# Graph attention and expert FFN in one kernel: each chunk is routed directly behind its finishing, and source columns are queued ahead of destination rows

## The chip, the cores and the metric

The kernel runs as one program on one core of one Trainium2 chip. The core has five engines with an instruction stream each: PE (TensorE, matmuls and transposes), DVE (VectorE), ACT (ScalarE), POOL (GpSimd) and SP (SyncE, here only an issuer of DMAs). They meet only at semaphores. The metric is the device time of one execution in microseconds (us), lower is better.

## The reference

One layer has two halves. The first is a graph attention over N = 6250 nodes of D = 256 features, with 106,250 edges sorted by destination (each node has a loop). The inner function adds its own loops again.

```
xl  = layernorm(x)
q   = tanh(xl @ Wq + bq);  k = xl @ Wk + bk              # 25 columns each
w   = sum(q[s] * k[d]) / 5                                # one number per edge s -> d
ew  = exp(w - segment_max(w, d)[d]);  alpha = ew / segment_sum(ew, d)[d]
x   = x + segment_sum(alpha * xl[s], d)
```

The second is a mixture of eight experts, two per node:

```
xn = layernorm(layernorm(x)) * gamma + beta;  logits = xn @ Wr + br
the two best experts of each node, softmax over their two logits -> w_full
x  = x + sum over e of w_full[e] * (gelu(xn @ W1[e] + b1[e]) @ W2[e] + b2[e])
```

## The kernel before, in words

**Stages.** From 0 to about 100 us the kernel normalises all rows, makes q and k, writes rows of 282 numbers (features, a one, q) to `rows_dram`, and computes on the chip a list of *items*. Then comes the edge stage, about 100 to 1233 us, and then the experts, which go over blocks of 256 gathered nodes.

**An item** is two groups of 512 consecutive edges, one for each half of the nodes, each with a window of 64 destination nodes. There are 106 items. For each one:
- SP loads its 2 x 512 source numbers, column-shaped, into `idx` (`load_sources`, L357, from `srccol` on chip) and its 512 destination numbers, spread over 64 partitions twice, into `dstb` (`load_targets`, L362, from `dst_dram`). Both have XSLOTS = 4 slots.
- POOL gathers the source rows with eight indirect DMAs (L539) into one of the four slots of `xg`.
- ACT copies q out (L1240), PE transposes it (L1442), ACT copies back (L1245), PE makes scores against the keys (L1451), DVE adds the mask and takes the maximum (`maximum`, L856, L861, L868), ACT makes exponentials (L1249), PE transposes them (L1458), ACT copies (L1255), PE sums the gathered rows with them (`sums`, L1466), and DVE scales and adds into `acc` (`add_sums`, L879).
- DVE makes the mask of the *next* item behind each maximum (`edge_mask`, L846) and adds the sums of the item *before*.

In the steady order PE's sums of item n stand behind the scores of item n+1, so they come out one item late. `PEEL = 2` items are done ahead of the loops; the rest goes in quads of four items, each a loop body.

**What frees what.** A gather of item n waits for its `idx` (semaphore `s_idx`) and for the sums of item n-4 (`s_pv`), which free the slot of `xg`. An `idx` slot is free when the gather of the item that used it has landed (`s_g`). A `dstb` slot is free when the mask of its item is made (`s_mask`).

**Chunks.** The nodes lie in NCH = 7 chunks of 7 x 128. Since edges are sorted by destination, a chunk is complete after some quad; `segment(c)` loads the first and last quad of chunk c from a table that the kernel computed. DVE, PE and ACT each run a loop over chunks 0 to 5, and the last chunk follows in plain code:

```
for c in 0..5:   quads lo..hi-1;  finished(c);  one quad (hi);  route(c)
last chunk:      quads lo..hi-1;                finished(6);    route(6)
```

The line numbers of a chunk on DVE: `finished` (L904 to L930) divides `acc` by its ones column, adds x (`xr`), takes statistics, normalises into `rows`, and waits for PE's router logits (L930 adds their bias). `route` (L950 to L1020) takes the top two of eight, counts the positions of the nodes in the lists of the experts with PE's help, and adds into the list `ltok` by 14 pairs of one-hot tiles (`ab`, `bb`, L1011, L1012) that PE multiplies (L1543). On PE `finished` is transposes and logits (L1513, L1519), and at its end PE waits for L930; at the end of `route` it waits for L1020. On ACT `finished` makes the inverse deviation, copies transposes, and stores the rows of the first half of the layer (L1285, L1287); `route` makes one exponential (L1312) and stores the normalised rows (L1294); `next_rows` loads the x rows of the next chunk (L1278 to L1281) and stands between quad and `route`.

PE does the sums of the last item ahead of a stop at once (`last_sums`), and the first item of the quad behind it has no sums to do (`fresh_quad`). DVE's addition for that last item is made in the next quad.

POOL and SP have no chunks: they run one loop over all quads and are held by semaphores alone. SP's quad, which the change edits:

```
sp.wait_ge(s_mask, number(s + 1));   load_targets(sp, s, group, s + XSLOTS)
sp.wait_ge(s_g[s], ...);             load_sources(sp, s, group, s + XSLOTS)
```

Of the kernel before, what the change touches and what calls it, by code (L numbers as in the profile page):

```python
# [62 lines left out]
XSLOTS = 4  # L63
PEEL = 2
# [24 lines left out]
def build(nc, x, src, dst, Wq, bq, Wk, bk, gamma, beta, Wr, br, W1, b1, W2, b2, out):  # L89
    ctx = ExitStack()  # L90
    with ctx:
# [178 lines left out]
        s_db = [sem(f"s_db{i}") for i in range(XSLOTS)]  # L270
# [31 lines left out]
        def kept(eng, value, low, high):  # L302

            return eng.snap(eng.to_reg(value), donate=True, min_val=low, max_val=high)
# [50 lines left out]
        def load_sources(eng, s, group, a):  # L355
            for x_ in range(2):
                eng.dma_start(idx[:, s, x_, :], srccol[:, bass.ds(group(x_, a), 1), :].rearrange("p o g -> p (o g)"))\  # L357
                    .then_inc(s_idx[s], 16)

        def load_targets(eng, s, group, a):  # L360
            for x_ in range(2):
                eng.dma_start(dstb[HP * x_:HP * x_ + HP, s, :],  # L362
                              dst_dram[bass.ds(group(x_, a) * GE, GE)].partition_broadcast(HP)).then_inc(s_db[s], 16)
# [15 lines left out]
        def _(sp):  # L379
# [34 lines left out]
            sp.wait_ge(s_m0, 1)  # L414
            sp.wait_ge(s_kb, NT)
            sp.wait_ge(s_d16w, 16)
            for s in range(PEEL, XSLOTS):
                load_targets(sp, s, group, s)

            sp.dma_start(xr[0:HP, :, :], x_tiles(x, 0, CH)).then_inc(a_x, 16)  # L420
            sp.dma_start(xr[HP:P, :, :], x_tiles(x, HALF, CH)).then_inc(a_x, 16)
# [4 lines left out]
            def quad(k):  # L426
                number = counter(sp, k)
                _, _, group = item_reader(sp, k)
                for s in range(XSLOTS):
                    sp.wait_ge(s_mask, number(s + 1))  # L430
                    sp.sem_inc(tk_s, 1)
                    load_targets(sp, s, group, s + XSLOTS)
                    sp.wait_ge(s_g[s], sp.to_reg(k * (32 * G) + 32 * G))
                    sp.sem_inc(tk_s, 1)
                    load_sources(sp, s, group, s + XSLOTS)

            n_quads = quad_count(sp)
            with sp.Fori(0, n_quads) as k:
                quad(k)

            n_items = kept(sp, n_quads * 4 + PEEL, NG // 2, ITEMS)
            sp.wait_ge(s_acc, n_items + 2)
            sp.sem_inc(tk_s, 1)
            for s in range(XSLOTS):
                sp.wait_ge(s_db[s], sp.to_reg(n_quads * 32 + 32))
                sp.sem_inc(tk_s, 1)
                sp.wait_ge(s_idx[s], sp.to_reg(n_quads * 32 + 32))
                sp.sem_inc(tk_s, 1)
# [158 lines left out]
        def _(v):  # L607
# [17 lines left out]
            v.memset(ltok[:, :], 0.0).then_inc(s_v0, 1)  # L625
            v.memset(kT[:, NT * P:NTX * P], 0.0).then_inc(s_v0, 1)
            v.sem_inc(s_acc, 2)

            def statistics_0(c):

# [392 lines left out]
            with v.Fori(0, NCH - 1) as c:  # L1023
                lo, hi = segment(v, c)
                with v.Fori(lo, hi) as k:
                    quad(k)
                v.wait_ge(s_acc, v.to_reg(hi * 4 + 3))
                v.sem_inc(tk_v, 1)
                finished(c)
                with v.Fori(hi, hi + 1) as k:  # L1030
                    quad(k)
                route(c)
            lo, hi = segment(v, NCH - 1)
            with v.Fori(lo, hi) as k:
                quad(k)
# [97 lines left out]
        def _(a):  # L1133
# [162 lines left out]
            def finished(c):  # L1296


                for h, (lo_, hi_) in enumerate(((0, FIRST_PART), (FIRST_PART, CH))):
                    a.wait_ge(a_mv, CH * c + hi_)  # L1300
                    nc.scalar.activation(lnv[:, 0, lo_:hi_], mv[:, 0, lo_:hi_, 1], ACT.Ln, bias=epsc[:, 1:2], scale=1.0 + EPS)\
                        .then_inc(a_ln, 1)
                    a.wait_ge(a_ln, c * 2 + h + 1)
                    nc.scalar.activation(rstd[:, 0, lo_:hi_], lnv[:, 0, lo_:hi_], ACT.Exp, scale=-0.5).then_inc(a_rs, 1)
                for u in range(CH):
                    a.wait_ge(a_tp, c * CH + u + 1)
                    nc.scalar.copy(xnT[:, u % 2, :, :].rearrange("p c n -> p (c n)"), pb[4 + u % 2][:, 0:D]).then_inc(a_ev, 1)
                store_x2(c)

            def route(c):  # L1310
                a.wait_ge(a_df, c + 1)
                nc.scalar.activation(ex[:, :], tdiff[:, :], ACT.Exp).then_inc(a_ex, 1)  # L1312
                store_normal(c)
# [7 lines left out]
            with a.Fori(0, NCH - 1) as c:  # L1321
                lo, hi = segment(a, c)
                with a.Fori(lo, hi) as k:
                    quad(k)
                finished(c)
                with a.Fori(hi, hi + 1) as k:
                    quad(k)
                next_rows(c)
                route(c)
            lo, hi = segment(a, NCH - 1)  # L1330
            with a.Fori(lo, hi) as k:
                quad(k)
# [36 lines left out]
        def _(pe):  # L1369
# [124 lines left out]
            def fresh_quad(lo):  # L1494

                with pe.Fori(lo, lo + 1) as k:
                    quad(k, fresh=True)
# [50 lines left out]
            with pe.Fori(0, NCH - 1) as c:  # L1548
                hi = segment_quads(c)
                last_sums(PEEL + 3, counter(pe, pe.snap(hi - 1)))  # L1550
                finished(c)
                fresh_quad(hi)
                last_sums(PEEL + 3, counter(pe, hi))
                route(c)
            segment_quads(NCH - 1)
            n_items = kept(pe, quad_count(pe) * 4 + PEEL, NG // 2, ITEMS)
            sums(1, 1, pe.to_reg(n_items), pe.to_reg(n_items))
# [69 lines left out]
```

## Time and profile before

| | us |
|---|---|
| median of 3 runs | 1678.6 (1676.88 to 1678.79) |
| the profiled execution, own time | 1678.56 |
| its span | 1676.8 |
| DVE's last finishing starts (edge stage over) | 1232.73 |

| engine | busy us | share of span |
|---|---|---|
| PE | 1124.2 | 67% |
| POOL | 1101.1 | 66% |
| DVE | 827.7 | 49% |
| ACT | 519.4 | 31% |

No engine is busy all the time, and the shares mix stages: PE is at 0.9 and more in the expert stage (about the last quarter) and at 0.5 to 0.6 in the edge stage, where POOL is at 0.7 and more. POOL's busy time does not count the 0.30 us that lie between one gather and the next, so for an engine with many short instructions the busy share understates how full it is. An engine's waits are listed with their releaser; "issue" is idle time with no releaser in the profile.

### The profile page before, as it was taken

How to read it: one execution, taken by the hardware profiler on the slowest of the kernel's cores; microseconds unless marked ns; L12 is line 12 of the kernel's file. 1: busy time of each engine (PE TensorE's matmuls, PEld its weight loads, DVE VectorE, ACT ScalarE, POOL GpSimd, SP SyncE). 2: the span in 40 equal slices, each digit the busy share in tenths (PEclk: the TensorE clock that was granted, in tenths of full speed). 3: DMA queues.
4: the chain of work that ended last, by engine and by line, in shares of the span. 5: the costliest groups of instructions: out<-in, count | busy, mean ns of one | idle time of the engine just before them, and what ended most of it. 6: DMA issues, size and time to landing. Idle time of an engine off the chain costs nothing.

```text
span 1676.8 us, 30544 instructions
## 1 busy us (share of the span) xinstructions
PE 1124.2 (67%) x6718; PEld 767.1 (46%) x6719; DVE 827.7 (49%) x3273; ACT 519.4 (31%) x1474; POOL 1101.1 (66%) x1099
## 2 busy tenths in 40 slices
PE   5935655655665665556565656555647999999997
PEld 5922332423342333234232423232335888888886
DVE  7724444565466545655664565457553232322322
ACT  2522222322232323233232213222322333434332
POOL 2047777767776777677677766777703667766675
PEclk9997656666566756666676566666767999999999
DMA  9475444555456445555544564456442454544543
GB/s 200 98 170 131 129 127 128 148 145 131 129 143 159 131 127 146 150 134 143 155 130 127 141 163 113 128 147 163 124 135 44 92 98 67 99 96 94 98 69 63
DMA packets 155748, 210.05 MB, mean 125 GB/s; under 512 B 59525, under 2 KB 122589, under 8 KB 155558
## 3 DMA queue, kind: packets, MB, share of 16 engines
q0 software_dynamic: 61360, 151.84, 37.4%
q1 hardware_dynamic: 73217, 38.82, 9.7%
q10 hardware_dynamic: 21110, 18.79, 4.4%
q14 instruction: 49, 0.40, 0.1%
q8 instruction: 12, 0.20, 0.0%
HBM read 174.49 MB, written 34.41 MB: 125 GB/s over the span
## 4 chain that ended last, share of the span: by engine, by line
PE 38%; POOL 21%; issue 16%; DVE 11%; DMA 7%; DVEq 4%; ACT 3%; ACTq 1%; POOLq 0%; SPq 0%
POOL arena_a L539 20%; PE pb L1595 9%; PE pb L1587 8%; PE pb L1466 6%; DMA arena_a<-rows_dram,idx 3%; PE pb L1519 2%; PE pb L1390 2%; DVEq L314 2%; DMA arena_b<-xn_dram,gidx 2%; PE pb L1451 2%; DMA out_dram<-arena_b,tokB 2%; PE pb L1513 2%; PE pb L1442 2%; PE pb L1572 1%; PE pb L1543 1%
## 5 line engine op out<-in xcount | busy, mean ns | idle before, releaser
L539 POOL DMA_INDIRECT arena_a<-rows_dram,idx x848 | 814.3, 960 | 380.7 <-issue 257.1
L1466 PE MATMUL pb<-arena_a,arena_b 128*64 128x257 f32 x1696 | 329.9, 557 | 12.8 <-ACT arena_b L1255 12.8
L1442 PE MATMUL pb<-ident,qs 128*128 128x128 f32 x212 | 64.1, 398 | 289.5 <-ACT qs L1240 262.7
L879 DVE SCALAR_TENSOR_TENSOR acc<-acc,alpha,pb 32x257 f32 x424 | 203.3, 480 | 77.3 <-issue 67.6
L1466 PEld LDWEIGHTS pb<-arena_a,arena_b 128*64 128x64 f32 x1696 | 159.9, 196 | 142.7 <-issue 112.1
L597 POOL DMA_INDIRECT out_dram<-arena_b,tokB x104 | 166.3, 1599 | 86.0 <-DVE arena_b L1121 65.7
L1587 PE MATMUL pb<-arena_b 128*128 128x256 f32 x832 | 190.5, 383 | 1.2 <-ACT arena_b L1345 1.2
L1595 PE MATMUL pb<-arena_b 128*128 128x256 f32 x832 | 188.2, 379 | 0.0
L861 DVE CUSTOM_DVE_ANT_0 arena_b<-pb,mask,nmo 128x512 f32<-128x512 f32 x106 | 79.6, 751 | 212.5 <-PE pb L1451 203.7
L1442 PEld LDWEIGHTS pb<-ident,qs 128*128 128x128 f32 x212 | 27.5, 182 | 323.4 <-ACT qs L1240 294.1
L1587 PEld LDWEIGHTS pb<-arena_b 128*128 128x128 f32 x832 | 159.7, 192 | 23.7 <-ACT arena_b L1345 1.6
L1363 ACT ACTIVATE arena_b<-pb,b1e 128x256 f32<-128x256 f32 x208 | 98.7, 474 | 224.2 <-PE pb L1587 224.2
L1595 PEld LDWEIGHTS pb<-arena_b 128*128 128x128 f32 x832 | 154.0, 190 | 18.8
L574 POOL DMA_INDIRECT arena_b<-xn_dram,gidx x108 | 108.0, 1000 | 74.6 <-DVE gidx L1056 30.0
L1112 DVE TENSOR_TENSOR arena_b<-pb,arena_b 128x256 f32<-128x256 f32 x104 | 39.3, 420 | 222.8 <-PE pb L1595 222.8
L1249 ACT ACTIVATE arena_b<-arena_b,nbias 128x512 f32<-128x512 f32 x106 | 76.5, 721 | 224.5 <-DVE nbias L861 222.9
L1458 PE MATMUL pb<-ident,arena_b 128*128 128x128 f32 x424 | 96.9, 370 | 45.4 <-ACT arena_b L1249 44.9
L1458 PEld LDWEIGHTS pb<-ident,arena_b 128*128 128x128 f32 x424 | 62.9, 186 | 108.8 <-ACT arena_b L1249 56.5
L846 DVE TENSOR_SCALAR mask<-arena_b,win_node 64x512 bf16<-64x512 int16 x214 | 77.6, 363 | 68.4 <-issue 65.9
L1451 PE MATMUL pb<-qT,kts 25*64 25x128 f32 x1696 | 71.5, 405 | 58.6 <-ACT qT L1245 58.6
L1240 ACT COPY qs<-arena_a 128x200 f32<-128x200 f32 x106 | 38.9, 367 | 199.4 <-DMA arena_a<-rows_dram,idx 154.9
L856 DVE COPY nmo<-nm_all 32x1 f32 x424 | 61.5, 145 | 75.0 <-issue 67.7
(221 smaller groups left out, 1264.5 us busy)
## 6 DMA issues: line engine op xcount, KB each, us to landing
arena_a<-rows_dram,idx POOLq DMA_INDIRECT x848
arena_b<-dst_dram SPq DMA_DIRECT2D x212, 64.0 KB
arena_b<-in_L_ffn_W_dram SPq DMA_DIRECT2D x16, 512.0 KB, 5.0
rows_dram<-acc SPq DMA_DIRECT2D x14, 493.5 KB, 6.0
xn_dram<-arena_a ACTq DMA_DIRECT2D x7, 910.0 KB, 8.7
acc<-in_x_dram SPq DMA_DIRECT2D x13, 448.0 KB, 13.9
out_dram<-arena_a ACTq DMA_DIRECT2D x13, 448.0 KB
idx<-srccol SPq DMA_DIRECT2D x214, 2.0 KB
```

The lines of the kernel that those rows point to most:

```text
L539: g.indirect_dma_start(out=xg[:, (s * 2 + x_) * G + j, :], out_offset=None, in_=rows_dram[:, :], in_offset=bass.IndirectOffsetOnAxis(ap=id ...
L574: g.indirect_dma_start(out=xrows[:, k, :], out_offset=None, in_=xn_dram[:, :], in_offset=bass.IndirectOffsetOnAxis(ap=gidx[:, k:k + 1], ax ...
L597: g.indirect_dma_start(out=out[:, :], in_=ybuf[:, k, :], in_offset=None, out_offset=bass.IndirectOffsetOnAxis(ap=tokB[:, k:k + 1], axis=0) ...
L861: v.tensor_tensor_reduce(out=sc[:, b, :].rearrange("p (j n) -> p j n", j=G), in0=score_banks[:, :, :], in1=mask[:, b, :].rearrange("p (j n ...
L879: ins = v.scalar_tensor_tensor(out=mine, in0=mine, scalar=alpha[rows_of, b:b + 1], in1=sums_bank[b][rows_of, 0:W1COLS], op0=ALU.mult, op1= ...
L1363: nc.scalar.activation(hT[:, m, :], hidden_bank[m][:, 0:ST], ACT.Gelu, bias=b1e[:, m:m + 1]).then_inc(b_g, 1)
L1442: last = nc.tensor.transpose(pb[0][:, x_ * P:(x_ + 1) * P], qs[:, x_, :, :].rearrange("p j s -> p (j s)"), ident[:, :])
L1451: last = mm(score_banks[HP * x_:HP * x_ + HP, j, :], kts[band, HP * x_:HP * x_ + HP], qT[band, x_, :], start=True, stop=True)
L1458: last = nc.tensor.transpose(pb[2][:, j * P:(j + 1) * P], sc[:, b, j * P:(j + 1) * P], ident[:, :])
L1466: last = mm(sums_bank[b][HP * x_:HP * x_ + HP, 0:W1COLS], probT[:, b, j * P + HP * x_:j * P + HP * x_ + HP], xg[:, (s * 2 + x_) * G + j, 0 ...
L1587: last = mm(hidden_bank[m][:, 0:ST], w1s[:, b, c, m * P:(m + 1) * P], xT[:, c, :], start=c == 0, stop=c == 1, skip_group_check=True)
L1595: last = mm(pb[3 + k2][:, 0:D], hT[:, c, k2 * P:(k2 + 1) * P], w2s[:, b, c, :], start=c == 0, stop=c == 3)
```

## The change

The change has two parts.

1. On DVE, ACT and PE, `route(c)` moves to directly behind `finished(c)`. The quad that stood between them comes behind both. ACT's `next_rows(c)` stays behind the quad. The last chunk is as before.
2. On SP, each step of a quad first waits for gather n and loads source columns of item n+4, and then waits for the mask that frees a slot and loads destination rows of item n+2 (before: destination rows of item n+4, then source columns of item n+4). The mask count starts at 2, so that the same number n+1 stands for the mask of item n-2. The loads of items 2 and 3 ahead of the loop go, the loop makes them, and one load is made behind the loop; the counts waited for at the end follow.

```diff
@@ SP
             sp.wait_ge(s_d16w, 16)
-            for s in range(PEEL, XSLOTS):
-                load_targets(sp, s, group, s)
...
                 for s in range(XSLOTS):
-                    sp.wait_ge(s_mask, number(s + 1))
-                    sp.sem_inc(tk_s, 1)
-                    load_targets(sp, s, group, s + XSLOTS)
                     sp.wait_ge(s_g[s], sp.to_reg(k * (32 * G) + 32 * G))
                     sp.sem_inc(tk_s, 1)
                     load_sources(sp, s, group, s + XSLOTS)
+                    sp.wait_ge(s_mask, number(s + 1))
+                    sp.sem_inc(tk_s, 1)
+                    load_targets(sp, (s + PEEL) % XSLOTS, group, s + PEEL)
...
+            sp.wait_ge(s_mask, counter(sp, n_quads)(1))
+            sp.sem_inc(tk_s, 1)
+            _, _, group = item_reader(sp, n_quads)
+            load_targets(sp, PEEL, group, PEEL)
...
-                sp.wait_ge(s_db[s], sp.to_reg(n_quads * 32 + 32))
+                sp.wait_ge(s_db[s], sp.to_reg(n_quads * 32 + (32 if s <= PEEL else 0)))
@@ DVE
             v.sem_inc(s_acc, 2)
+            v.sem_inc(s_mask, PEEL)
...
                 finished(c)
+                route(c)
                 with v.Fori(hi, hi + 1) as k:
                     quad(k)
-                route(c)
@@ ACT
                 finished(c)
+                route(c)
                 with a.Fori(hi, hi + 1) as k:
                     quad(k)
                 next_rows(c)
-                route(c)
@@ PE
                 finished(c)
+                route(c)
                 fresh_quad(hi)
                 last_sums(PEEL + 3, counter(pe, hi))
-                route(c)
```

Line numbers of DVE, ACT and PE code are higher by 3 in the changed kernel (L930 is L933, L950 is L953).

On DVE, before the change, the end of `finished` (L930) stands directly ahead of the quad's loop (L1030), whose first work is the `nmo` copies of `maximum`:

```order
L930 TENSOR_TENSOR lg<-pb,lbias 128x56
L1030 UNCONDITIONAL_BRANCH
L1030 ISA
L314 ISA
L314 TENSOR_LOAD item_row
```

And the end of `route` (L1020) stands ahead of the jump back to the head of the chunk loop (L1023) and the loads of the segment's bounds:

```order
L1017 TENSOR_TENSOR ltok<-ltok,pb 128x408
L1020 TENSOR_TENSOR ltok<-ltok,xnT 128x408
L1023 REGISTER_ALU
L1023 COMPARE_AND_BRANCH
L341 TENSOR_LOAD segl
L341 ISA x2
L342 TENSOR_LOAD segh
```

In the changed kernel the end of `finished` (L933) is followed by the first rows of `route`:

```order
L933 TENSOR_TENSOR lg<-pb,lbias 128x56
L953 MAX top<-lg 128x8 x7
L955 ISA
L956 TENSOR_TENSOR tdiff<-top 128x7
L958 MAX_INDEX topi<-top,lg 128x8 x7
```

and the end of `route` (L1023) by the quad's loop (L1034):

```order
L1020 TENSOR_TENSOR ltok<-ltok,pb 128x408
L1023 TENSOR_TENSOR ltok<-ltok,xnT 128x408
L1034 UNCONDITIONAL_BRANCH
L1034 ISA
L314 ISA
L314 TENSOR_LOAD item_row
L314 ISA x2
```

What moved is the whole of `route`, 77 rows, over the quad; the jump back and the segment's bounds now stand behind the quad.

On SP, a step of the quad loop before the change (`arena_b<-dst_dram` are destination rows, `idx<-srccol` source columns; two of each, one per half):

```order
L304 REGISTER_ALU [waits s_mask]
L304 REGISTER_ALU
L362 ISA
L362 DMA arena_b<-dst_dram 64x512
L304 REGISTER_ALU x2
L362 ISA
L362 DMA arena_b<-dst_dram 64x512
L357 ISA [waits s_g1]
L357 DMA idx<-srccol 128x4
L357 ISA
L357 DMA idx<-srccol 128x4
```

and the same step after it:

```order
L304 REGISTER_ALU [waits s_g1]
L304 REGISTER_ALU
L357 ISA
L357 DMA idx<-srccol 128x4
L304 REGISTER_ALU x2
L357 ISA
L357 DMA idx<-srccol 128x4
L351 REGISTER_ALU
L304 REGISTER_ALU [waits s_mask]
L304 REGISTER_ALU
L362 ISA
L362 DMA arena_b<-dst_dram 64x512
```

The two pairs of DMAs have changed places with their waits.

## Rows read from the trace of the kernel before

**Rows 1.** The page: shares of the chain that ended last, and the gathers' group.

```profile
POOL arena_a L539 20%; PE pb L1595 9%; PE pb L1587 8%; PE pb L1466 6%; DMA arena_a<-rows_dram,idx 3%; PE pb L1519 2%; PE pb L1390 2%; DVEq L314 2%; DMA arena_b<-xn_dram,gidx 2%; PE pb L1451 2%; DMA out_dram<-arena_b,tokB 2%; PE pb L1513 2%; PE pb L1442 2%; PE pb L1572 1%; PE pb L1543 1%
...
L539 POOL DMA_INDIRECT arena_a<-rows_dram,idx x848 | 814.3, 960 | 380.7 <-issue 257.1
```

**Rows 2.** Waits, 240 to 1260 us: engine line, waited for, total us, times, longest us.

```profile
POOL arena_a L539 <- issue: 224.2, 715, 1.9
...
POOL arena_a L539 <- PE pb L1466: 44.3, 23, 7.8
```

**Rows 3.** Timeline of POOL: start us, duration us, instruction, [idle before <- releaser].

```profile
321.93 0.95 POOL L539 DMA_INDIRECT arena_a<-rows_dram,idx  x1 [0.30 <-issue]
324.40 0.95 POOL L539 DMA_INDIRECT arena_a<-rows_dram,idx  x1 [1.52 <-PE pb L1466]
...
371.56 0.95 POOL L539 DMA_INDIRECT arena_a<-rows_dram,idx  x1 [6.66 <-PE pb L1466]
374.38 0.95 POOL L539 DMA_INDIRECT arena_a<-rows_dram,idx  x1 [1.86 <-issue]
...
1133.41 0.95 POOL L539 DMA_INDIRECT arena_a<-rows_dram,idx  x1 [1.47 <-PE pb L1466]
```

**Rows 4.** Timeline of DVE, the first chunk's two stops.

```profile
290.66 1.96 DVE L879 SCALAR_TENSOR_TENSOR acc<-acc,alpha,pb 32x257 f32 x4
...
309.31 0.21 DVE L930 TENSOR_TENSOR lg<-pb,lbias 128x56 f32<-128x56 f32 x1 [7.05 <-PE pb L1519]
...
313.85 0.75 DVE L861 CUSTOM_DVE_ANT_0 arena_b<-pb,mask,nmo 128x512 f32<-128x512 f32 x1 [0.22 <-DVE nmo L856]
...
333.49 0.75 DVE L861 CUSTOM_DVE_ANT_0 arena_b<-pb,mask,nmo 128x512 f32<-128x512 f32 x1 [0.95 <-PE pb L1451]
...
336.83 1.96 DVE L879 SCALAR_TENSOR_TENSOR acc<-acc,alpha,pb 32x257 f32 x4
338.83 0.57 DVE L950 MAX8 top<-lg 128x8 f32<-128x8 f32 x7
...
353.43 0.58 DVE L1020 TENSOR_TENSOR ltok<-ltok,xnT 128x408 f32<-128x408 f32 x1
359.34 0.30 DVE L856 COPY nmo<-nm_all 32x1 f32 x2 [5.33 <-issue]
...
361.04 0.75 DVE L861 CUSTOM_DVE_ANT_0 arena_b<-pb,mask,nmo 128x512 f32<-128x512 f32 x1 [0.22 <-DVE nmo L856]
```

**Rows 5.** Timeline of DVE, the last chunk, finished and routed in one stop.

```profile
1232.73 0.20 DVE L904 RECIPROCAL rl<-acc 128x7 f32<-128x7 f32 x1
...
1248.60 0.22 DVE L930 TENSOR_TENSOR lg<-pb,lbias 128x56 f32<-128x56 f32 x1 [7.05 <-PE pb L1519]
1248.96 0.57 DVE L950 MAX8 top<-lg 128x8 f32<-128x8 f32 x7
...
1263.04 0.58 DVE L1020 TENSOR_TENSOR ltok<-ltok,xnT 128x408 f32<-128x408 f32 x1
```

**Rows 6.** Timeline of SP's queue, the first chunk's finishing.

```profile
294.85 1.18 SPq L357 DMA_DIRECT2D idx<-srccol  x2
316.52 1.35 SPq L362 DMA_DIRECT2D arena_b<-dst_dram  x2
318.10 1.19 SPq L357 DMA_DIRECT2D idx<-srccol  x2
```

**Rows 7.** The page, DMA issues: count, KB each, median us from issue to landing.

```profile
xn_dram<-arena_a ACTq DMA_DIRECT2D x7, 910.0 KB, 8.7
```

**Rows 8.** Windows: us, busy us by engine (instructions), PE clock granted, DMA share, GB/s.

```profile
309.50:324.40 14.90, 8.43 (x60) 4.40 (x60) 7.62 (x30) 5.05 (x18) 10.33 (x12) 0.51 0.66 189
324.40:338.80 14.40, 10.11 (x92) 5.59 (x92) 10.57 (x36) 5.82 (x19) 11.05 (x12) 0.88 0.47 124
354.00:371.56 17.56, 8.49 (x60) 4.45 (x60) 7.88 (x31) 4.70 (x16) 8.46 (x9) 0.50 0.33 91
1248.90:1263.60 14.70, 6.92 (x22) 1.81 (x22) 13.13 (x73) 1.49 (x2) 0.00 (x0) 0.50 0.40 120
```

## The prediction, made blind

> **What bounds the kernel now.** I read the page first. The chain that ended last gives 20% to POOL at line L539, more than to any other line, and L539 is 848 gathers of 0.96 us [rows 1]. Each gather starts 0.30 us after the one before it ends, so an item, which has eight, costs POOL about 8 x 1.257 = 10.06 us. I then read the waits of the middle stretch (240 to 1260 us): POOL waited for the "sums" matmuls (L1466) 44.3 us in 23 waits, and the other 224.2 us are the 0.30 us steps between gathers [rows 2]. The steps are in those 23 waits too, so what POOL really lost there is 44.3 - 23 x 0.30 = 37.4 us. The middle stretch is therefore POOL's gathers back to back, plus 37.4 us. Everything else in that stretch is hidden.
>
> Where the 37.4 us lie is read in POOL's timeline [rows 3]. In the first chunk there is a wait of 1.52 us before the gather at 324.40, in the quad behind `finished`, and one of 6.66 us before 371.56, behind `route`. Later chunks repeat it: five of six have the small one (1.46 to 1.52 each, 1.2 above the step; the last is shown), one has none. So finishing costs about 6.0 us in all and routing 37.4 - 6.0 = 31.4 us.
>
> Why the first is so small: with four slots in `xg`, the gather of item n waits for the sums of item n-4. When compute stops behind the sums of item L, POOL may still fetch L+1 to L+4. VectorE's timeline [rows 4] has its last sums of the chunk end at 290.66 + 1.96 = 292.62, and POOL would have been free for item L+5 at 321.93 + 0.95 + 0.30 = 323.18 [rows 3]. **The lead is 30.6 us.** Finishing takes 292.62 to 309.52 (the end of L930), and from there to the gather that its restart releases, at 324.40, it is 14.9 us. Together 31.8, 1.2 more than the lead. The lead is already spent by finishing alone, before a routing of 15 us is put in it.
>
> Between the two stops, the quad gives some lead back. Its items go at (333.49 - 313.85) / 3 = 6.5 us against POOL's 10.06 [rows 4]. So the quad that stands between the stops is not just there for order: it is what lets POOL's next four slots open early, and routing then costs 5.2 us of POOL (mean) though it holds compute for 15.2.
>
> **The change part by part.** (1) The order of finishing, quad and routing, on DVE, PE and ACT, six times. The last chunk had no quad between and stays as it is.
>
> Added: in one stop DVE ends finishing, then routes, then restarts. Routing on DVE runs from 338.83 to 353.43 + 0.58 = 354.01, 15.18 us [rows 4]. That the two run straight after each other without gaining or losing is seen in the last chunk, which already does it [rows 5]: L930 ends at 1248.82, routing starts at 1248.96 and ends at 1263.62, 14.66 us (code without loop registers). I take 0.14 for the seam and 15.18 for routing. The restart is the one behind finishing, 14.9 us from the end of DVE's stop to POOL's gather. The one behind routing now takes 371.56 - 354.01 = 17.55, of which DVE's first maximum starts 7.03 behind the stop instead of 4.33 [rows 4]. What stood between was the jump back to the top of the chunk loop and the loading of the next segment's bounds; in the changed order that jump is behind the quad, so I take 14.9 and keep 17.55 as the other end. The stop then runs 292.62 + 16.9 + 0.14 + 15.18 + 14.9 = 339.7 where the first release is 324.40 now: 15.3 us later. POOL has nothing else to do from 323.18 on, so it is lost in full: 6 x 15.3 = **+91.9 us**.
>
> Removed: the six waits behind routing, **-31.4 us**, if nothing is late in their place. What would be is the seam from the quad to the next segment, with the jump back. Take the release of the first gather as t = 0. DVE's last sums of the quad end at 336.83 + 1.96 - 324.40 = 14.4; with the long restart of 17.55 the next segment's first sums are out at 32. POOL needs them after four items, at 40.2. Eight us are left, so it costs nothing. ScalarE's loads of the next x rows (`next_rows`) fall in the same seam: they were issued there before and stand in this slack too. The store of the routed rows now precedes the quad on ACT's queue; it waits for VectorE early in routing, and PE holds ScalarE until routing ends anyway.
>
> (2) SP's order: source columns of item n+4 before destination rows of item n+2, the latter issued later than before. POOL's waits of the middle stretch are for sums or have no releaser; none is for source columns [rows 2]. At the stop the columns of L+5 were issued at 294.85 [rows 6], 28 us before POOL could use them. SP then stood until 316.52 at the mask wait, and issued the next columns at 318.10, when POOL needs them ten us behind 324.40. Both are hidden, so loading them earlier gains 0. The destination rows are the risk. They now go out behind the landing of gather n for item n+2, whose mask is made in item n+1 behind its maximum: one POOL period (10.06) plus some 5 us later, less 2.5 us of issuing (1.18 and 1.35) [rows 6]. That leaves about 12 us to land 64 KB. No row gives its landing time, but a store of 910 KB lands in 8.7 us [rows 7], so 0 is taken, between 0 and the 12 us that would have to be exceeded. The two loads taken out of the start and the one put behind the loop are hidden by the same 12 us.
>
> **Sum.** +91.9 - 31.4 = +60.5 us. On the profiled execution, 1676.8 of span and 1678.56 of its own time, that is 1739.1; its own time is the median shown (1678.6), so the forecast is **1739**. Two small things are left as spread: in four of the loops POOL's second gather comes 1.86 instead of 0.30 us late (the one at 374.38 is shown) [rows 3], for no reason that I can read, so that 6 us may come or go; and chunk 2 had 0 to spare rather than -1.2. The case's own range is 1731 to 1747.
>
> **Rivals.** A: the restart behind routing stays long, because it hangs on code behind routing and not on the jump back. Then 2.65 more in each stop, 6 x 2.65 = 16, time **1755**. For it: the 5.33 us that DVE needs before L856 has no releaser in the profile [rows 4]. Against: finishing falls straight into a quad without it.
>
> B: TensorE stays awake over the joined stop and restarts at full rate. In both kinds of restart the granted clock is 0.50 to 0.51, its lower level of 1.2 GHz, and in the quad behind 0.88, mostly 2.4 GHz [rows 8]. PE is busy 8.43 us in the first restart. If the part of it on the chain went at the rate of the quad, I estimate 3 us off the 14.9 (half of 8.43, less what overlaps), 6 x 3 = 18, time **1721**. Against it: in the last chunk, where the two stops are already joined, the clock reads 0.50 all through routing [rows 8]. The Trainium skill (TensorE: Matmul & The Clock Gate, Part 1: "the default state is throttled, and activity releases the throttle") names the mechanism that B would need, and by it the joined stop, with no quad of waiting items before the restart, would end at the higher rate; in this trace the releases come inside the quads and not in the last chunk's routing, so the rule keeps a small chance.
>
> C, the other side: one stop instead of two saves a whole restart and POOL's four-item lead carries it. All waits behind L1466 would go, -37.4, time **1641**. It decides at the lead: end of sums to first release must stay under 30.6 us for all of it, and under 30.6 + 6.2 = 36.8 not to be slower. The joined stop is 47.1. Ten us would have to vanish from rows that follow each other on DVE, and nothing in the change shortens them.
>
> D: no change that can be told, because POOL's lead is longer than I read, or what is lost at the joined stop was lost at two before: **1679**. Against it the lead is fixed by four slots and 10.06 us each.
>
> E: a new wait, destination rows that land behind their mask or the quad-to-segment seam going over its 8 us. Say 5 us in six seams, 30 more: **1769**.
>
> **Chances.** Forecast 0.74, A 0.12, B 0.05, C 0.03, D 0.02, E 0.04. A difference of 0.2%, 3.4 us, is about what can be told from no change. Slower is the forecast, A, B and E: 0.95. Same 0.02, faster 0.03. The range reaches from the forecast's low end a little toward B and up to A: 1728 to 1757 holds the forecast and A, 0.86, less what the ends may miss.
>
> **What would show it.** POOL's waits for L1466 in the middle stretch should read six of about 16.5 us each above the step, about 98 us in all, at the first gather of each quad behind routing, and none of 5 or more elsewhere. DVE should go from L933 to L953 within 0.2 us and from there to L1023 in 15.2. The stretch from DVE's last routing row to POOL's next gather should be 14.9, and 17.5 if A holds; TensorE's clock there 0.50, and near 1 if B holds. SP's waits for the mask should shrink in favour of waits for gathers, with POOL never waiting for `idx`. The front (to 280 us) and the expert part (behind the last gather) should keep their lengths. POOL waits under 6 us per chunk, or the gather of L+5 starting before 330, would make the forecast wrong at its root; so would any DVE wait for destination rows at the mask line.

## The result, and the profile after

The changed kernel takes 1716.7 us (median; 1715.3 to 1720.2 in 4 runs) where the kernel before takes 1678.5 in the same comparison (1676.9 to 1678.8, 4 runs): a ratio of 1.0242, 95% interval 1.0225 to 1.0259, or 38.2 us more. The direction was forecast. The size was not: 1739 was said, with 1728 as the lowest. Of the 24 executions of the kernel before that ran beside e1 to e4 below, one took 2121.3 us and one 1789.6, and two of the six of e8 were slower than its others (2189.3 and 2193.3); the ratios leave these four out.

The profiled execution has 1715.26 us of its own time and a span of 1713.5. In the page of the changed kernel the gathers are L541 and stay the first group on the chain. Columns are as in [rows 1]:

```profile
POOL arena_a L541 25%; PE pb L1598 9%; PE pb L1590 8%; PE pb L1469 6%; DMA arena_a<-rows_dram,idx 4%; PE pb L1522 2%; PE pb L1454 2%; DMA arena_b<-xn_dram,gidx 2%; PE pb L1516 2%; PE pb L1445 1%; PE pb L1546 1%; DMA out_dram<-arena_b,tokB 1%; PE pb L1575 1%; DVE st L919 1%; ACT qT L1248 1%
...
L541 POOL DMA_INDIRECT arena_a<-rows_dram,idx x848 | 813.5, 959 | 417.2 <-issue 253.3
```

The gathers themselves cost what they cost before (813.5 us); the idle time ahead of them grew from 380.7 to 417.2, which is 36.5 of the 36.7 us that the span grew (the wait ahead of the first gather, 78.94 and 71.24, is in both). The waits of POOL in the middle stretch, 240 to 1290 us, columns as in [rows 2]:

```profile
POOL arena_a L541 <- issue: 220.1, 712, 1.9
POOL arena_a L541 <- PE pb L1469: 91.1, 21, 14.7
```

POOL lost 91.1 - 21 x 0.30 = 84.8 us to the sums, against 37.4 before [rows 2]: +47.4, where the forecast had +60.5. They lie in six waits, one per joined stop. POOL's timeline at the first two:

```profile
331.15 0.95 POOL L541 DMA_INDIRECT arena_a<-rows_dram,idx  x1 [14.74 <-PE pb L1469]
332.41 0.95 POOL L541 DMA_INDIRECT arena_a<-rows_dram,idx  x1 [0.30 <-issue]
...
506.82 0.95 POOL L541 DMA_INDIRECT arena_a<-rows_dram,idx  x1 [13.79 <-PE pb L1469]
509.63 0.95 POOL L541 DMA_INDIRECT arena_a<-rows_dram,idx  x1 [1.86 <-issue]
```

The other four read 14.74, 14.74, 14.22 and 14.26. The reader is to see one long wait where [rows 3] has a short and a middling one. The odd 1.86 us ahead of a second gather is there in two chunks instead of four: -3.1 us.

The first joined stop in DVE's timeline answers to [rows 4]:

```profile
286.23 0.20 DVE L907 RECIPROCAL rl<-acc 128x7 f32 x1 [0.27 <-DVE acc L882]
...
302.74 0.22 DVE L933 TENSOR_TENSOR lg<-pb,lbias 128x56 f32<-128x56 f32 x1 [7.01 <-PE pb L1522]
303.10 0.51 DVE L953 MAX8 top<-lg 128x8 f32<-128x8 f32 x6
...
317.39 0.58 DVE L1023 TENSOR_TENSOR ltok<-ltok,xnT 128x408 f32<-128x408 f32 x1
318.72 0.30 DVE L859 COPY nmo<-nm_all 32x1 f32 x2 [0.74 <-issue]
319.88 0.31 DVE L859 COPY nmo<-nm_all 32x1 f32 x2 [0.87 <-issue]
320.57 0.75 DVE L864 CUSTOM_DVE_ANT_0 arena_b<-pb,mask,nmo 128x512 f32<-128x512 f32 x1 [0.38 <-PE pb L1454]
```

Finishing runs from the last sums (285.96) to 302.96, 17.0 us; routing follows 0.14 later and ends at 317.97, 14.87 long; the first maximum starts 2.60 us behind the stop; POOL is released at 331.15, 13.18 behind it. The windows of the three parts, columns as in [rows 8]:

```profile
285.96:302.96 17.00, 10.14 (x54) 8.90 (x50) 8.63 (x30) 3.61 (x11) 12.92 (x14) 0.65 0.50 127
302.96:317.97 15.01, 7.07 (x22) 1.81 (x22) 13.25 (x72) 0.57 (x2) 10.40 (x11) 0.50 0.83 246
317.97:331.15 13.18, 8.48 (x60) 4.45 (x60) 7.70 (x31) 4.63 (x16) 0.00 (x0) 0.50 0.06 15
```

TensorE's granted clock in the restart is 0.50, the lower level (1.2 GHz), as in both restarts of before. POOL is idle in the whole of it.

The first gather starts at 94.25 us, against 101.25 before, so 7.0 us come from the front of the kernel, which the change does not touch. Together: +47.4 - 3.1 - 7.0 = +37.3, against 36.7 measured on the span.

### The profile page after: what moved, and what is told of

The parts are those of the page before. It is cut to its first block, busy times and chain, and to the rows that moved or that the text cites. A ratio compares the mean times of both kernels' runs of the same rounds, so it can differ in the third digit from the quotient of the medians.

```text
span 1713.5 us, 30969 instructions
## 1 busy us (share of the span) xinstructions
PE 1123.7 (66%) x6718; PEld 758.2 (44%) x6719; DVE 826.6 (48%) x3273; ACT 520.6 (30%) x1474; POOL 1100.4 (64%) x1099
## 3 DMA queue, kind: packets, MB, share of 16 engines
q0 software_dynamic: 61360, 151.84, 37.3%
## 4 chain that ended last, share of the span: by engine, by line
PE 35%; POOL 25%; issue 17%; DVE 10%; DMA 7%; ACT 3%; DVEq 1%; ACTq 1%; POOLq 1%; SPq 0%
POOL arena_a L541 25%; PE pb L1598 9%; PE pb L1590 8%; PE pb L1469 6%; DMA arena_a<-rows_dram,idx 4%; PE pb L1522 2%; PE pb L1454 2%; DMA arena_b<-xn_dram,gidx 2%; PE pb L1516 2%; PE pb L1445 1%; PE pb L1546 1%; DMA out_dram<-arena_b,tokB 1%; PE pb L1575 1%; DVE st L919 1%; ACT qT L1248 1%
## 5 line engine op out<-in xcount | busy, mean ns | idle before, releaser
L541 POOL DMA_INDIRECT arena_a<-rows_dram,idx x848 | 813.5, 959 | 417.2 <-issue 253.3
L1469 PE MATMUL pb<-arena_a,arena_b 128*64 128x257 f32 x1696 | 338.1, 568 | 12.1 <-ACT arena_b L1258 12.1
L1461 PE MATMUL pb<-ident,arena_b 128*128 128x128 f32 x424 | 96.6, 369 | 36.5 <-ACT arena_b L1252 36.5
```

Source lines behind the costliest of these rows:

```text
L541: g.indirect_dma_start(out=xg[:, (s * 2 + x_) * G + j, :], out_offset=None, in_=rows_dram[:, :], in_offset=bass.IndirectOffsetOnAxis(ap=id ...
L1461: last = nc.tensor.transpose(pb[2][:, j * P:(j + 1) * P], sc[:, b, j * P:(j + 1) * P], ident[:, :])
L1469: last = mm(sums_bank[b][HP * x_:HP * x_ + HP, 0:W1COLS], probT[:, b, j * P + HP * x_:j * P + HP * x_ + HP], xg[:, (s * 2 + x_) * G + j, 0 ...
```

## The experiments

Four batches were run (e1 to e4, e5 to e8, e9 to e12, e13 to e16), each on a chip of its own with the kernel before beside it. In the second and third the kernel before itself took 2128 us; the sections on them say what was different there. Their verdicts are read against that kernel.

### The two parts apart: SP's order alone, the joined stop alone

e1 has SP's new order and the stops of before; e2 has the joined stop and SP's old order (columns behind rows). The core of e2:

```
                 finished(c)
+                route(c)
                 with v.Fori(hi, hi + 1) as k:
                     quad(k)
-                route(c)
```

> Only SP's new order (sources ahead, destination rows two items ahead), stops as before. Theory (all of the loss is in the joined stop): no change, 1678 +- 3. Rival (the new order itself shortens the front, since the changed kernel's first gather came at 94.25 instead of 101.25 us): the first gather at about 94 and 1671. Rival (destination rows land late at the mask): 1690 and more.

> Only the joined stop, SP's order as before. Theory: six waits of POOL for L1466 of about 14.4 us each in place of the 37.4 us in all, so +47, less whatever the front does; 1716 to 1726 depending on whether the first gather starts at 94 or 101 us. Rival (SP's order is what lets the restart behind routing be short, since the mask wait no longer holds the source columns): the waits are 16 to 17 us each and the time 1735 to 1740.

e1: 1680.3 us (1675.5 to 1682.7, 12 runs), ratio 1.0021, 1.0005 to 1.0037. Its waits behind finishing and routing are those of before (1.83 and 6.73 in the first chunk). SP's order alone does not gain: it costs 3.5 us by the medians' ratio (0.8 to 6.2), of which POOL's waits for the sums show 2.5 (47.7 us in 26 waits, 39.9 above the step, against 37.4). POOL never waited for source columns. e2: 1718.9 us (1717.9 to 1720.9), ratio 1.0258, 1.0227 to 1.0290. Its six waits are 14.01 to 14.74, the first of them:

```profile
333.84 0.95 POOL L539 DMA_INDIRECT arena_a<-rows_dram,idx  x1 [14.74 <-PE pb L1466]
```

With SP's old order the loss is as large as in the changed kernel, and the short restart is there too: the loss is the joined stop's.

### A shorter routing inside the joined stop

e3 is the changed kernel with the routing of chunks 0 to 5 cut: 4 of its 14 one-hot pairs (L1014, L1015) are made, the rest is left out, so the routed lists of those chunks are incomplete.

```
-                for u in range(CH):
+                for u in range(CH if last else 2):
```

> The changed kernel with the first 4 of the 14 one-hot pairs in the routing of chunks 0 to 5 (the other ten are left out, so the lists of the experts lack nodes of these chunks). Routing on DVE gets shorter by ten pairs of 0.47 us, 4.7 us. Theory (POOL's lead of 30.7 us is overspent, so each us of the stop is a us of the kernel): each of the six waits falls from 14.4 to about 9.7, time -28, about 1689. Rival (the stop is paid by something other than the lead, the clock or the restart): less than -10.

1688.3 us (1686.1 to 1692.6), ratio 1.0077, 1.0050 to 1.0104 to the kernel before. Routing is 303.55 to 313.68, 10.1 us instead of 14.9, and the waits are 10.06 to 10.55, where about 9.7 were expected:

```profile
303.55 0.58 DVE L953 MAX8 top<-lg 128x8 f32<-128x8 f32 x7
...
313.10 0.58 DVE L1023 TENSOR_TENSOR ltok<-ltok,xnT 128x408 f32<-128x408 f32 x1
```

```profile
326.86 0.95 POOL L541 DMA_INDIRECT arena_a<-rows_dram,idx  x1 [10.35 <-PE pb L1469]
```

A routing 4.7 us shorter gives 4.1 us less wait at each stop (from 91.1 to 66.7 us in all) and 28.4 us less time than the changed kernel in its own comparison, 30.6 less than e2 beside it. Six times 4.7 is 28.4: beyond the lead, a microsecond of stop is about a microsecond of kernel. The stretch behind the last gather is as long as before (460.8 and 460.9 us of span), so the shorter lists do not blur this.

### Why the restart is shorter than forecast

The restart was taken from behind finishing (14.9), but in the joined stop it is 13.2. The suspicion: behind finishing, ACT issues two stores ahead of its first copy `qs`. The trace of before, ACT's rows behind the first finishing, and DVE's:

```profile
308.04 0.77 ACTq L1285 DMA_DIRECT2D out_dram<-arena_a  x1
309.00 0.68 ACTq L1287 DMA_DIRECT2D out_dram<-arena_a  x1
309.95 0.37 ACT L1240 COPY qs<-arena_a 128x200 f32<-128x200 f32 x1 [1.77 <-issue]
```

```profile
311.46 0.30 DVE L856 COPY nmo<-nm_all 32x1 f32 x2 [1.94 <-issue]
313.33 0.31 DVE L856 COPY nmo<-nm_all 32x1 f32 x2 [1.57 <-issue]
```

In the changed kernel these stores are issued at 301.47 and 302.44, ahead of the routing, and the same two gaps of DVE are 0.74 and 0.87. e4 is the kernel before with the stores (`store_x2`) at the end of routing and `next_rows` behind it; nothing is joined.

```
-                store_x2(c)          (end of finished, ACT)
...
+                store_x2(c)          (end of route, ACT)
-                next_rows(c)
                 route(c)
+                next_rows(c)
```

> The kernel before, with ACT's two stores of x rows moved from the end of finishing to the end of routing, and the loads of the next x rows behind them. The restart behind finishing takes 14.9 us, the one behind the joined routing 13.2. Theory (the restart behind finishing is long because ACT issues these two stores ahead of the first copy and because their traffic slows DVE's loads of item registers, 1.57 instead of 0.87 us): the first maximum starts about 2.6 to 3.3 us behind L930 instead of 4.33, POOL's small waits of 1.2 us go, time -3 to -7 unless the routing stop grows by the loads. Rival (it is the order of the code or the place of the instructions that sets it): 4.33 stays, and the time.

1680.9 us (1677.4 to 1686.1, 10 runs), ratio 1.0030, 1.0013 to 1.0047. Behind finishing there is no wait at all any more. ACT's `qs` starts at 308.07, and DVE:

```profile
310.61 0.30 DVE L856 COPY nmo<-nm_all 32x1 f32 x2 [1.09 <-issue]
311.77 0.31 DVE L856 COPY nmo<-nm_all 32x1 f32 x2 [0.86 <-issue]
312.30 0.75 DVE L861 CUSTOM_DVE_ANT_0 arena_b<-pb,mask,nmo 128x512 f32<-128x512 f32 x1 [0.22 <-DVE nmo L856]
```

The first maximum is 2.78 us behind the stop instead of 4.33, which is 1.55 of the missing 1.73 us. It is not ACT's late copy that did it. PE's scores, which hang on that copy, had long been made in the kernel before when DVE's maximum started at 313.85:

```profile
311.61 0.73 PE L1451 MATMUL pb<-qT,kts 25*64 25x128 f32 x16 [0.55 <-ACT qT L1245]
```

The maximum waited for the `nmo` copies, and what got shorter are the two gaps ahead of these, from 1.94 + 1.57 to 1.09 + 0.86, 1.56 us in sum. In the gaps DVE branches and loads registers (L1030, L314). The DMA share between stop and maximum is 0.86 in the kernel before, 0.41 in e4 and 0.09 in the joined stop; that the transfers slow DVE's register loads fits this, but was not tested by itself.

But the loads now stand ahead of the restart behind routing, and the gain is given back there and more (POOL's waits for the sums are 43.4 us above the step, against 37.4):

```profile
354.65 0.30 ACTq L1281 DMA_DIRECT2D arena_a<-in_x_dram  x1
357.05 0.37 ACT L1240 COPY qs<-arena_a 128x200 f32<-128x200 f32 x1 [17.55 <-issue]
```

```profile
361.06 0.30 DVE L856 COPY nmo<-nm_all 32x1 f32 x2 [7.63 <-issue]
```

The waits behind routing become 9.32, 6.6, 8.7, 8.23, 9.42 and 2.84. Expected were 3 to 7 us less of time, unless the loads lengthen the stop at routing, and this is what they did. e7, and again e11 and e15, put the stores ahead of the routing and the loads behind it:

> The kernel before, with ACT's two stores of x rows moved from the end of finishing to behind the quad, ahead of routing, and the loads of the next x rows behind routing. e4 (stores inside routing) had no wait behind finishing any more, but restarted 2.3 us later behind routing, since ACT issued the next loads from 352.12 to 354.95. With the stores 6 us earlier they land earlier and the loads should be out before 350. Theory: no waits behind finishing (-6), those behind routing as before or 1 to 2 us better each: 1664 to 1671. Rival (something else lengthened the restart behind routing in e4): waits behind routing of 8 to 9 us, 1680.

> The kernel before, ACT storing x2 behind the quad ahead of the routing and loading the next rows behind the routing. Theory (ACT's issues ahead of its first copy lengthen a restart by about 1.7 us): no wait behind finishing (1.6 to 1.9 us before), the waits behind routing no longer than 7 us; 1666 to 1676. Rival (the issues only move the delay to the other stop, as with the stores behind routing): waits behind routing of 8 to 9 us, 1676 to 1682.

> The kernel before, ACT storing x2 behind the quad ahead of the routing, next rows loaded behind the routing. Theory (issues ahead of ACT's first copy lengthen a restart; a stop at which ACT issues nothing has the short one, a stop at which it does the long one): behind finishing no wait; behind routing 7 to 9 us since the loads are issued there; time 1672 to 1682. Rival (restart independent of ACT's issues): waits as in the kernel before, within 0.3 us each.

Where an item takes 10.06 us (e15): 1682.2 us (1678.9 to 1686.6, 10 runs), ratio 1.0036, 1.0019 to 1.0053. Again no wait behind finishing, where the maximum is 2.76 behind L930, and 8.3 to 10.0 behind routing in five chunks (expected were 7 to 9, and 1682 at most). Near whichever stop ACT issues transfers, the restart is longer, as the theory said, but not by the way it named. In e15 ACT has issued the loads 5 us before DVE's routing ends (345.86) and made its first copy 3 us before; DVE's gap is the longer all the same, 8.27 against 5.33:

```profile
340.38 0.30 ACTq L1281 DMA_DIRECT2D arena_a<-in_x_dram  x1
342.79 0.37 ACT L1240 COPY qs<-arena_a 128x200 f32<-128x200 f32 x1 [11.05 <-issue]
```

```profile
354.13 0.30 DVE L856 COPY nmo<-nm_all 32x1 f32 x2 [8.27 <-issue]
```

On the two other chips e7 and e11 were level with the kernel before (0.9984, 0.9955 to 1.0013, and 0.9976, 0.9946 to 1.0006); for both less time had been expected, 1664 to 1671 and 1666 to 1676, on a chip like the first.

### What stands between two stops: one quad or two

If the lead of four items is what hides a stop, then a second quad between finishing and routing should make it whole again. PE's loop needed a new form for that, in which the last sums are taken at the end of each pass; e5, e9 and e13 have that form alone, e6, e10 and e14 two quads with it, e8 also the stores of e7. With two quads the table of segments is changed to match, so that the next segment starts one quad later.

```
-                with v.Fori(hi, hi + 1) as k:
+                with v.Fori(hi, hi + 2) as k:
                     quad(k)
                 route(c)
```

> The kernel before with PE's sums of a quad's last item done at the quad's end in every quad (before: only ahead of a stop), so that each quad starts without sums to do. It is the ground for the next kernel. Theory (in the steady quads POOL's gathers set the pace, compute has 3 us per item to spare): no change, 1677 +- 4, POOL's waits for the sums as before (37 us in all). Rival (the break at each quad costs compute more than it has to spare): 20 quads of 2 us or more, 1710 and up.

> e5 with two quads between finishing and routing in place of one. Theory (the quad between the stops gives lead back, 3.5 us per item; after two of them the lead is full, and routing with its restart takes 15.2 + 17.55 = 32.7 us of a lead of 30.6): the six waits behind routing fall from 31.4 us in all to 6 x 2.1 = 13, so 18 less than e5, about 1659. Rival (one quad gives back all that is to be had): no change against e5. Rival (lead isn't what decides, the number of restarts is): no change.

> e6 and e7 together. Theory (both are terms of the same lead and add up): about 1652 to 1656, POOL's waits for the sums under 15 us in all. Rival (they overlap, since the small wait behind finishing delays POOL's slots that the routing then uses): no better than e6.

> The kernel before, with TensorE's last sums taken at the end of each of its loops' passes instead of at the start of the next; beside it the kernel before ran at about 2128 us in the earlier batch, where POOL waited some 2.8 us for each item, so the question is put again. Theory (the lead of 30 us covers what one pass ends later): within 0.3% of the kernel before, 1677 +- 5. Rival (the sums at the end of a pass stand in the way of the next item's products and POOL is held): +1.5% or more, as in the earlier batch.

> The kernel of e9 with two quads instead of one between a chunk's finishing and its routing. Theory (POOL is held behind a stop by what the stop, its restart and the gap before the next stop leave beyond the lead of four items; two quads, 80 us of gathers, let the lead grow whole again before the routing): the waits behind routing fall from 6 to 7.5 us to under 2, six times about 5, so 1660 to 1668 if e9 is level with the kernel before. Rival (the lead is four items and is filled within one quad anyway, the wait behind routing is the routing's own 15 us plus its restart): as e9, within 0.3%.

The first two rounds fell on the chips with 2128 us. There e5 had 1.0167 (1.0127 to 1.0206), e6 1.0187 (1.0145 to 1.0229), e8 1.0166 (1.0129 to 1.0204), e9 1.0241 (1.0178 to 1.0304), e10 1.0194 (1.0130 to 1.0259): the new form costs 1.7 to 2.4%, and two quads give nothing that can be told. The expectations for e5, e6, e8 and e10 missed, and of e9's two the rival came. So the question was put a third time:

> The kernel before, with TensorE's last sums taken at the end of every pass of its loops. Where an item takes 10.06 us on POOL: theory (each end of a pass makes the sums of an item about 3 us later or earlier, within the lead): within 0.3% of the kernel before, 1675 to 1683. Rival (each end of a pass stops PE, ACT and DVE for 8 to 10 us, as in the slower batches, and the lead is not whole when a stop comes): waits behind finishing of more than 4 us, +0.5 to +2%.

> The kernel of e13 with two quads between finishing and routing. Theory (the wait behind routing is 30.1 us of routing and restart less a lead that one quad leaves 1 to 5 us short, since the finishing used it up): the waits behind routing 2 to 6 us shorter than in e13, the time 12 to 36 us under e13. Rival (the lead is whole within one quad): waits and time as in e13, within 5 us.

On a chip where an item takes 10.06 us, e13 is level with the kernel before: 1678.6 us (1671.6 to 1683.6, 10 runs), ratio 1.0006, 0.9988 to 1.0025. e14 takes 1658.6 us (1652.1 to 1660.8, 4 runs), ratio **0.9891**, 0.9860 to 0.9921. It is the fastest kernel of the study, and its slowest run is 10.8 us under the fastest of e13. POOL's waits of the middle stretch, e13 and then e14:

```profile
POOL arena_a L539 <- PE pb L1466: 46.3, 17, 7.8
```

```profile
POOL arena_a L539 <- PE pb L1466: 20.9, 13, 4.0
```

And the first of e14 behind a routing, where before it was 6.66 [rows 3]:

```profile
399.02 0.95 POOL L539 DMA_INDIRECT arena_a<-rows_dram,idx  x1 [2.13 <-PE pb L1466]
```

The waits fall by (46.3 - 5.1) - (20.9 - 3.9) = 24.2 us, the medians by 20.1. The prediction had the routing and its restart at 15.2 + 17.55 = 32.7 us against a lead of 30.6; with a whole lead 2.1 would be left, and that is about what e14 shows behind routing: 1.96 to 2.13 us in five chunks, each with the step of 0.30 in it, and none in the sixth. The rest of its waits stand behind finishing, 1.1 to 1.7 in four chunks and 4.01 in one. In e13 the waits behind routing are 6.5 to 7.8 in four chunks, 4.67 in one and 1.86 in the sixth, so one quad did leave the lead some 3 to 6 us short in five chunks.

### The changed kernel where POOL has less lead

> The changed kernel once more, for what its profile showed beside the longer waits: its first gather started 7 us earlier than in the kernel before. Theory (the front of the kernel, which the change does not touch, varies by some us between executions with TensorE's granted clock): the first gather anywhere in 94 to 101 us, the six waits 13.8 to 14.8 us again, the time 1712 to 1722 and its distance to the kernel before 36 to 44. Rival (the change shortens the front): the first gather at 94 to 95 again.

e12 is the changed kernel on one of the chips with 2128 us: 2129.4 us (2112.6 to 2136.0, 10 runs), ratio 0.9994, 0.9956 to 1.0032. The expected 1712 to 1722 did not come, and the change costs nothing there that can be told (-9 to +7 us). POOL's waits, 400 to 1200 us:

```profile
POOL arena_a L541 <- PE pb L1469: 189.1, 11, 34.7
POOL arena_a L541 <- issue: 121.7, 374, 1.9
POOL arena_a L541 <- remote: 106.8, 38, 4.1
```

and its timeline over a few items:

```profile
506.67 0.95 POOL L541 DMA_INDIRECT arena_a<-rows_dram,idx  x1 [2.93 <-remote]
519.46 0.95 POOL L541 DMA_INDIRECT arena_a<-rows_dram,idx  x1 [3.02 <-remote]
532.40 0.96 POOL L541 DMA_INDIRECT arena_a<-rows_dram,idx  x1 [3.16 <-remote]
545.13 0.95 POOL L541 DMA_INDIRECT arena_a<-rows_dram,idx  x1 [2.84 <-remote]
```

An item takes 12.2 to 12.9 us instead of 10.06, and POOL stands before nearly every one. Its lead is shorter: in the second chunk DVE's last sums end at 599.50 and POOL is free for the next item at 651.63 - 34.69 + 0.30 = 617.24, 17.7 us later instead of 30.8. Finishing is longer too, to 623.79, 24.3 us instead of 17.0. So most of a stop is paid, wherever it stands. In e12 the joined stops cost POOL 32.0 to 34.7 us each, and the seam behind the quad, which is hidden on the other chips, 12.2 to 13.9 more in five chunks, together about 47. In e11, with two stops, it is 15 to 16 in most chunks behind finishing (22.6 in one) and 27 to 31 behind routing, about 45 in most. That the quad between the stops gives only what the lead can take fits these sums, but it is argued: the kernel before has no trace on these chips, and e11 differs from it by ACT's stores and loads.

> The changed kernel once more. Theory (the front varies with the execution, the change acts on the waits alone): first gather between 94 and 101 us; six waits of 13.8 to 14.8 us; 1712 to 1722, ratio 1.021 to 1.027. On a chip where POOL has no lead: ratio 0.995 to 1.004 as before, the sum of the two waits of a stop and the item behind it 46 us. Rival (the change shortens the front): first gather at 94 to 95.

e16 repeats the changed kernel beside e13 to e15: 1719.4 us (1716.6 to 1721.4), ratio 1.0243, 1.0212 to 1.0274, six waits of 14.04 to 14.74. Its first gather starts at 98.29. With the changed kernel the first gather has now been seen at 94.25, 93.98 (e12) and 98.29 us; with the kernel before at 101.25, and with others that keep its two stops at 98.98 (e1), 100.91 (e4), 92.49 (e11), 97.97 (e13), 93.45 (e14) and 95.04 (e15). The front varies by up to 9 us between executions, and the 7 us of the first comparison are not the change's.

## Why the prediction was wrong in size and right in kind

- **POOL's pace bounds the middle, and a lead of four items hides a stop up to 30.6 us.** Right, and now shown: the lead read 30.8 us in the changed kernel (331.15 - 14.74 + 0.30 - 285.96), wait and time followed the stop (e3, 4.1 us of wait and 4.7 of time for 4.7 of stop), and a second quad restored it (e14). With a lead of 17.7 us the place of the stop made no difference that could be told (e12).
- **Finishing 16.9, seam 0.14, routing 15.18.** Right: 17.0, 0.14, 14.87.
- **The restart of 14.9.** This is the step that failed: a term of the sum was too large. It was taken from behind finishing, as the nearest row. It measured 13.18 (12.66 to 13.18 at the other stops). In that row ACT issues two stores at the stop's end, from 308.04 on, and DVE's two gaps ahead of its `nmo` copies are 1.94 and 1.57 us; in the joined stop the stores lie ahead of routing, and the gaps are 0.74 and 0.87. e4 took the stores out of the old restart and got gaps of 1.09 and 0.86, with a maximum 2.78 us behind the stop (2.60 in the joined stop). How stores lengthen DVE's gaps stays open. The prediction had named the load of the next rows and the store of the routed rows on ACT's queue, but not the x2 stores. 1.7 us here and 0.3 in routing, six times: 12 of the 22 us; the waits as a whole came out 13.1 under the forecast.
- **The removed waits behind routing.** -31.4 was right: nothing came in their place, and the seam from the quad to the next segment was hidden on the chips with a lead.
- **SP's order worth 0.** Right in kind: it gains nothing and hides no stop. Alone it cost 3.5 us (e1); beside the joined stop e2 and e16 do not differ (1.0258 and 1.0243).
- **The front keeps its length.** The change does nothing to it that the runs show, but one execution differs from the next by up to 9 us, and the two that were compared by 7. The range had no term for this. With the 3 us of the 1.86 us gaps, which was left as spread, that is the rest of the error. The repeat e16 came to 1.0243 again, so the loss stands at 38 to 42 us and not at the forecast 60. That the first comparison came out at the low end is luck, as far as the one profile of each kernel tells: its front was the shorter.
- **The rivals.** A (the long restart of 17.55) fell: what lengthened it was the jump back. The trace of before could have told: behind the sixth routing the code runs straight on into the last chunk, DVE's gap is 2.17 us instead of 5.2 to 5.3, and the restart is 14.65.

```profile
1164.72 0.30 DVE L856 COPY nmo<-nm_all 32x1 f32 x2 [2.17 <-issue]
```

  B said 1721, near the result, but for a reason that did not occur: the clock in the restart is 0.50. Who had bet on B would have been right by luck. C, D and E did not occur; D's price did on the two chips with 2128 us, and its second reason, that what is lost at one stop had been lost at two before, fits the waits there.

## What to carry to other kernels

A producer with a fixed lead hides a stop of the consumer only once per refill: two stops must be spaced by enough consumer work to make the lead whole again, and joining them makes everything beyond the lead visible at full price. When a restart is priced from another place, list every instruction that each engine's queue issues around the stop and the restart, DMA issues included, and ask which of them go along; then read in the trace whose gap they lengthen, for here it was not that of the engine that issued them. And before a difference between two profiles is given to an edit, see whether a stretch that the edit cannot touch differs too.

## What the runs showed of the hardware that was not expected

- The front's length goes with the pace of PE's matmuls, and the granted clock recorded there does not always tell that pace. The windows of 70 to 75 us, of the kernel before, of e2 and of e14, columns as in [rows 8]:

```profile
70.00:75.00 5.00, 5.00 (x28) 5.00 (x27) 1.70 (x7) 3.12 (x10) 0.00 (x0) 1.00 0.64 140
```

```profile
70.00:75.00 5.00, 5.00 (x27) 4.93 (x26) 3.42 (x12) 1.81 (x5) 0.00 (x0) 0.50 0.70 158
```

```profile
70.00:75.00 5.00, 4.41 (x37) 3.72 (x37) 4.45 (x16) 3.54 (x12) 0.00 (x0) 1.00 0.64 141
```

  The transposes of L1379 among them last 430 ns in the kernel before, at a recorded 1.00, 430 in e2 at 0.50 and 277 in e14 at 1.00. So this part of the kernel before, recorded at the higher level, ran at the pace that e2 has at the lower one. Over 55 to 94 us about the same matmuls keep PE busy for 34.3 us in the kernel before and for 26.8 in the changed one, whose first gather comes 7.0 us earlier. Whether the record or the engine is at odds there is open; a granted clock is best read beside the duration of a matmul.
- On two of the four chips an item took 12.2 to 12.9 us with the same programs, the gather's own 0.96 us unchanged. POOL's wait in each item has no releaser in the profile ("remote"), and DVE's maximum starts 0.8 to 0.9 us ahead of POOL's gather (at 518.59, 531.63 and 544.36 in e12), 7 to 8 us behind the end of the score matmuls that it needs by the profile. What both wait for was not found, nor whether it belongs to the chip: one execution of the kernel before took 2121.3 us on the chip of e1 to e4 too, without a trace. It decides whether this change costs 2.4% or nothing.
- DVE needed 1.94 and 1.57 us ahead of its first two pairs of copies, where it branches and loads registers, just after ACT had issued two 448 KB stores, and 1.09 and 0.86 without them (before and e4). With the jump back in the gap it was 5.21 to 5.33, and 7.6 to 9.2 with ACT's loads near it (before, e4, e15).
